# Rows on partitions: a first pass that convolves on TensorE, wide operands in the clustering, and attention in factored form

## The chip, the cores and the metric

The kernel runs on one core of a Trainium2 chip. The metric is the device time of one execution in microseconds, the median of several executions. The engines are TensorE (PE, with its weight loads shown apart as PEld), VectorE (DVE), ScalarE (ACT), GpSimd (POOL) and SyncE (SP), whose queue issues all the DMAs here.

## What is computed

The input x is 8 images of 512 channels of 128x128 float32, 268 MB. Two layers follow each other.

```python
# layer 0
x = conv(sx, w_down, stride 2, padding 1, groups of 2 channels)     # 8 x 256 x 64 x 64
labels = kmeans(normalised x[0], K=8, 10 iterations)                # over the 256 channels
v5 = mean of x over the channels of each cluster                    # 8 x 8 x 64 x 64
mu, var = gmm_fit(v5)                                               # 10 EM steps
pre_up = gate[:, slabel] * x + x                                    # gate from mu, var, w_conv
out0 = bilinear_up_x2(repeat(pre_up, 2, axis=1) * w_up) + sx
# layer 1; P is (128*128) x 64: products of 8 row and 8 column cosines
xP = einsum('bcn,nk->bck', x2, P)
WqxP, WkxP, WvxP = Wq @ xP, Wk @ xP, Wv @ xP
lamdq, lamdk = norms over o of (WqxP @ P.T), (WkxP @ P.T)           # one for every position
A = P.T @ (P / lamdk)                                               # 64 x 64, a sum over 16384 positions
out = ((A @ fatt) @ (P.T / lamdq) + P.sum(0)) / lamdv
out = gamma * (WvxP @ out + out_bias) + x
```

## The kernel before

Four parts follow each other, each a scope that ends with a barrier of all engines. A group of two input channels is convolved with its own 2x3x3 weights. T = 2 halves of 128 groups lie on the 128 partitions, and S = 2 is the channel within a group.

`first_pass` (L116) reads every image half in four chunks of 32 rows, a load of 4 MB each (L156), whose rows in memory are 16 KB long. The 18 taps of the convolution are 18 passes over a chunk: ACT makes the first (L282), DVE the other 17 (L217, a multiply and add that reads every second element), but for half of the fourth chunk, which POOL makes (L197 and L202). Beside that PE turns each row of x with the identity (L316), ACT copies the turned rows out of PSUM (L289), and PE multiplies them by `p_cols` (L328), which gives xP, the projection on the 64 cosine products. The two row blocks of L328 are written to the two halves of the output partitions in turn. The convolved rows go to the DRAM tensor `downsampled` (L170).

`gather_pass` (L364) reads `downsampled` back (L433), takes the same projection of it with transposes (L648) and products (L658), and runs k-means on image 0: PE makes a Gram matrix (L602), and 11 iterations of three small steps (L616, L622, L627) are threaded between the transposes, by the position numbers `ITER_AT` and so on. A step reads 8 columns. The averages of the clusters follow (L686). SP also issues here, in a list named `later`, the loads of tables for later use (L443). `mixture_pass` fits the mixture, on small operands.

`second_pass` (L1071) goes through the images in units of 4 rows, two units to a chunk of 8 rows. In a unit PE turns the interpolated rows and the cosine rows (L1336, L1349), DVE and POOL scale the turned rows (L1147), PE makes 16 products (L1366), and DVE adds them to x (L1607). SP stores each chunk in two DMAs of 1 MB (L1188) and loads another, three chunks ahead (L1180), into the buffer that a store has left. The attention numbers of the next image (`stage`) are made in the gaps between the units. There DVE and PE work over all 16384 positions: `norm_rows`, `norm_columns` (L1256, L1262, with L1516, L1526, L1529 on DVE), then `over_lam` and `over_positions` (16 DVE products L1536, 128 PE products L1270). For the first image they stand alone, ahead of the first unit.

Of the kernel before, what the change touches and what calls it, by code (L numbers as in the profile page):

```python
# [31 lines left out]
for _name, _width in CONST_COLS:  # L32
    CONST_AT[_name] = slice(CONST_N, CONST_N + _width)
    CONST_N += _width

# [52 lines left out]
TAPS = [(s, dh, dw) for dw in (0, -1, 1) for dh in (-1, 0, 1) for s in range(S)]  # L88
ROWS1 = 32
CH1 = H // ROWS1  # L90
TAPS_LEFT = len(TAPS) - 1
OUT1 = ROWS1 // 2
QUADS = S * ROWS1 // 4
SLOTS = 4
TP_BANKS = 2
UNROLL1 = 4
POOL_CHUNK = 3
FIRST_TAPS = [0, QUADS, 2 * QUADS, 2 * QUADS + 2]
STEPS = [TAPS_LEFT, TAPS_LEFT, TAPS_LEFT, 2 * TAPS_LEFT]


def weight_of(s, dh, dw):

    k = s * 9 + (dh + 1) * 3 + dw + 1
    return slice(k, k + 1)


def tap_window(buf, tap, rows, row0=0):

    s, dh, dw = tap  # L110
    top = 1 + dh + 2 * row0
    left = dw if dw >= 0 else 1
    return buf[:, s, top:top + 2 * rows - 1:2, left:left + 2 * (WD - (dw < 0)) - 1:2]


def first_pass(nc, x, w_down, p_cols, consts, cst, xd, xps):  # L116

    xv = x.rearrange("b (t g s) h w -> (b t) g s (h w)", t=T, s=S)
    with Scope(nc, "first") as sc:
        xt = [sc.sb(f"x{c}", [P, S, ROWS1 + 1, W]) for c in range(CH1)]  # L120
        wd = sc.sb("wd", [P, T, S * 9])
        p_sb = sc.sb("p", [P, H, UV])
        acc = [sc.sb(f"acc{i}", [P, OUT1, WD]) for i in range(CH1)]
        xT = [sc.sb(f"xT{i}", [P, 4, P]) for i in range(SLOTS)]
        tp = [sc.ps(f"tp{i}", [P, 4, P]) for i in range(TP_BANKS)]
        freq_ps = [sc.ps(f"freq{t}", [P, 512]) for t in range(T)]
        sum_ps = [bank[:, S * P:S * P + S * UV] for bank in freq_ps]
        product = sc.sb("product", [P, OUT1 // 2, WD])
        partial = [sc.ps(f"partial{i}", [P, OUT1, WD]) for i in range(2)]
        halves = sc.sb("halves", [P, S * P])  # L130
        const_in, p_in = sc.sem("const_in"), sc.sem("p_in")
        x_in = [sc.sem(f"x_in{c}") for c in range(CH1)]
        pe_read = [sc.sem(f"pe_read{c}") for c in range(CH1)]
        top_zero = sc.sem("top_zero")
        started = sc.sem("started")
        tapped = [sc.sem(f"tapped{c}") for c in range(CH1)]
        upper_tapped = sc.sem("upper_tapped")
        stored = [sc.sem(f"stored{i}") for i in range(CH1)]
        transposed = sc.sem("transposed")
        copied = [sc.sem(f"copied{i}") for i in range(SLOTS)]  # L140
        multiplied = [sc.sem(f"multiplied{i}") for i in range(SLOTS)]
        freq_read, folded, sum_read = sc.sem("freq_read"), sc.sem("folded"), sc.sem("sum_read")
        ident, fold = cst[:, CONST_AT["ident"]], cst[:, CONST_AT["fold"]]
        quads = CH1 * QUADS

        with nc.Block() as block:
            @block.sync
            def _(sp):
                sp.dma_start(cst[:, :], consts).then_inc(const_in, 16)
                sp.dma_start(wd[:, :, :], w_down.rearrange("(t g) s a b -> g t (s a b)", t=T)).then_inc(const_in, 16)  # L150

                def load(i, c):

                    sp.wait_ge(pe_read[c], i + FREE)
                    above = 1 if c == 0 else 0
                    sp.dma_start(xt[c][:, :, above:, :].rearrange("g s h w -> g s (h w)"),  # L156
                                 xv[i, :, :, (c * ROWS1 - 1 + above) * W:(c + 1) * ROWS1 * W]
                                 ).then_inc(x_in[c], 16)

                for c in range(CH1):  # L160
                    load(0, c)
                    if c == 0:
                        sp.dma_start(p_sb[:, :, :], p_cols.rearrange("w (h k) -> w h k", k=UV)).then_inc(p_in, 16)

                def store(i, c):

                    sp.wait_ge(tapped[c], i * STEPS[c] + STEPS[c] + FREE)
                    if c == POOL_CHUNK:
                        sp.wait_ge(upper_tapped, i * TAPS_LEFT + TAPS_LEFT + FREE)
                    sp.dma_start(xd.rearrange("b t g n -> (b t) g n")[i, :, c * OUT1 * WD:(c + 1) * OUT1 * WD],  # L170
                                 acc[c][:, :, :].rearrange("g h w -> g (h w)")).then_inc(stored[c], 16)

                start_free(sp, stored)
                with sp.Fori(0, B * T - 1) as i:
                    for c in range(CH1):
                        store(i, c)
                        load(i + 1, c)
                for c in range(CH1):
                    store(B * T - 1, c)
                for c in range(CH1):  # L180
                    sp.wait_ge(stored[c], B * T * 16 + FREE)

            @block.gpsimd
            def _(pool):
                nc.gpsimd.memset(xt[0][:, :, 0, :], 0.0).then_inc(top_zero, 1)
                start_free(pool, [tapped[POOL_CHUNK]])
                c, rows = POOL_CHUNK, slice(OUT1 // 2, OUT1)
                for i in range(B * T):
                    done = i * STEPS[c] + FREE
                    pool.wait_ge(x_in[c], i * 16 + 16)  # L190
                    pool.wait_ge(started, i * CH1 + c + 1)
                    for n, (s, dh, dw) in enumerate(TAPS[1:]):
                        left = 1 if dw < 0 else 0

                        if n > 0 or i > 0:
                            pool.wait_ge(tapped[c], done + 2 * n)
                        nc.gpsimd.tensor_scalar(product[:, :, left:],  # L197
                                                tap_window(xt[c], (s, dh, dw), OUT1 // 2, OUT1 // 2),
                                                wd[:, i % T, weight_of(s, dh, dw)], None, ALU.mult
                                                ).then_inc(tapped[c], 1)  # L200
                        pool.wait_ge(tapped[c], done + 2 * n + 1)
                        nc.gpsimd.tensor_tensor(acc[c][:, rows, left:], acc[c][:, rows, left:], product[:, :, left:],  # L202
                                                ALU.add).then_inc(tapped[c], 1)

            @block.vector
            def _(dve):
                dve.wait_ge(top_zero, 1)
                start_free(dve, [*tapped[:3], upper_tapped])

                def tap(t, c, n, rows, mine):  # L210
# [847 lines left out]
PIECES = 16  # L1058
PKBUF = 4
FACTORS = UNITS - 3  # L1060
SET_UP = 5

# [718 lines left out]
```

## Time and profile before

| | us |
|---|---|
| median of 3 runs | 3322.35 (3321.49 to 3327.83) |
| profiled execution, its own time | 3323.32 |
| its span | 3321.5 |
| PE busy in the span | 2942.4 |
| DVE busy | 2716.8 |
| ACT busy | 1839.0 |
| POOL busy | 1431.5 |
| moved by DMA | 946.92 MB |

The span counts from the first instruction to the last one. Busy times are of whole stages and say nothing of what a stage waits for. For that the stages are taken one by one, by the engine and by the share of time in which the DMA engines had packets.

### The profile page before, as it was taken

What the parts mean: (1) busy time and instruction counts of PE and PEld (TensorE: products, weight loads), DVE (VectorE), ACT (ScalarE), POOL (GpSimd) and SP (SyncE); (2) the same over time, 40 slices, a digit from 0 to 9 for tenths busy, and PEclk for the clock granted to TensorE, in tenths of its full rate; (3) what the DMA queues carried; (4) which work ended last, traced back from release to release, by engine and by line L of the source; (5) the groups of instructions that cost most, each with busy time, mean ns of one, the idle gap of its engine ahead of it and who ended that gap; (6) DMA issues with size and microseconds to landing.
All of it is one profiled execution on the core that took longest, in us unless ns stands there. A gap on an engine that the chain in (4) does not pass through costs nothing. (4 is left out here: it accounts for less than half of the span.)

```text
span 3321.5 us, 62992 instructions
## 1 busy us (share of the span) xinstructions
PE 2942.4 (89%) x23398; PEld 2260.2 (68%) x23398; DVE 2716.8 (82%) x3454; ACT 1839.0 (55%) x4385; POOL 1431.5 (43%) x805
## 2 busy tenths in 40 slices
PE   6898989898899985998586899999999999999997
PEld 4565656565555553763343798888889898888887
DVE  4999999899999994110554898989999998989997
ACT  4455555555555554122231767676766767676675
POOL 1676766666677772000000334343343434334443
PEclk9899999899999997769797999999999999999999
DMA  6667666756556645245003799999999999999999
GB/s 266 262 257 283 245 248 262 278 227 268 233 233 249 274 190 199 102 181 194 6 0 146 279 372 391 377 383 386 377 384 371 390 374 390 375 382 390 377 412 392
DMA packets 190885, 946.92 MB, mean 285 GB/s; under 512 B 13505, under 2 KB 13633, under 8 KB 170626
## 3 DMA queue, kind: packets, MB, share of 16 engines
q1 hardware_dynamic: 190594, 943.04, 73.2%
q8 instruction: 183, 3.00, 0.4%
q14 instruction: 108, 0.88, 0.1%
HBM read 638.90 MB, written 301.99 MB: 283 GB/s over the span
## 5 line engine op out<-in xcount | busy, mean ns | idle before, releaser
L1147 POOL TENSOR_TENSOR second_left<-second_mid_copy,second_coef_rep 64x1024 f32<-64x1024 f32 x256 | 606.2, 2368 | 1435.6 <-ACT second_mid_copy L1473 1405.2
L1366 PE MATMUL second_o<-second_right,second_left 128*128 128x128 f32 x8192 | 1065.6, 278 | 84.9 <-issue 28.7
L1366 PEld LDWEIGHTS second_o<-second_right,second_left 128*128 128x128 f32 x8192 | 978.9, 192 | 138.8 <-issue 109.7
L217 DVE SCALAR_TENSOR_TENSOR first_partial<-first_x,first_wd,first_partial 128x1024 f32<-128x1024 f32 (+1 forms) x960 | 1015.6, 1175 | 0.0
L1607 DVE SCALAR_TENSOR_TENSOR second_x<-second_o,second_shift,second_x 128x512 f32<-128x512 f32 x1024 | 724.7, 736 | 121.9 <-PE second_o L1366 117.8
L289 ACT ACTIVATE first_xT<-first_tp 128x512 f32<-128x512 f32 x1024 | 566.8, 596 | 439.3 <-PE first_tp L316 437.0
L316 PE MATMUL first_tp<-all_const,first_x 128*128 128x128 f32 x4096 | 592.1, 288 | 137.2 <-ACT first_xT L289 91.9
L316 PEld LDWEIGHTS first_tp<-all_const,first_x 128*128 128x128 f32 x4096 | 454.7, 145 | 346.2 <-issue 227.0
L197 POOL TENSOR_SCALAR first_product<-first_x,first_wd 128x512 f32<-128x512 f32 (+1 forms) x272 | 465.5, 1712 | 415.7 <-ACT first_acc L282 390.5
L328 PE MATMUL first_freq<-first_xT,first_p 128*64 128x256 f32 x4096 | 565.5, 399 | 0.0
L202 POOL TENSOR_TENSOR first_acc<-first_acc,first_product 128x512 f32<-128x512 f32 (+1 forms) x272 | 359.3, 1321 | 22.7
L328 PEld LDWEIGHTS first_freq<-first_xT,first_p 128*64 128x64 f32 x4096 | 254.9, 139 | 166.6 <-issue 92.9
L1452 ACT ACTIVATE second_mid<-second_dd,all_inter 128x128 f32<-128x128 f32 x1024 | 313.3, 389 | 7.6 <-DMA second_dd<-downsampled 4.4
L1452 ACT ACTIVATE second_part<-second_dd,all_inter 128x128 f32<-128x128 f32 x1024 | 313.3, 389 | 3.2
L1147 DVE TENSOR_TENSOR second_left<-second_mid_t,second_coef_rep 64x1024 f32<-64x1024 f32 x256 | 308.7, 1206 | 0.9 <-PE second_mid_t L1336 0.6
L1473 ACT ACTIVATE second_mid_copy<-second_mid_t 64x512 f32<-64x512 f32 x256 | 151.7, 593 | 266.8 <-PE second_mid_t L1336 266.1
L566 ACT ACTIVATE gather_dT<-gather_tp 128x512 f32<-128x512 f32 x128 | 76.4, 598 | 202.1 <-PE gather_tp L648 201.9
L1588 DVE TENSOR_TENSOR second_mid<-second_mid,second_part 128x1024 f32<-128x1024 f32 x128 | 172.6, 1348 | 3.5 <-ACT second_part L1452 3.5
L1336 PE MATMUL second_mid_t<-all_const,second_mid 128*128 128x128 f32 x1024 | 161.0, 280 | 15.9 <-DVE second_mid L1588 15.9
L217 DVE SCALAR_TENSOR_TENSOR first_partial<-first_x,first_wd,first_acc 128x1024 f32<-128x1024 f32 x64 | 85.4, 1363 | 97.2 <-ACT first_acc L282 95.6
L1476 ACT ACTIVATE second_right<-second_zt_t 64x256 f32<-64x256 f32 x256 | 96.6, 377 | 119.9 <-PE second_zt_t L1349 119.2
L282 ACT ACTIVATE first_acc<-first_x,first_wd 128x512 f32<-128x512 f32 x128 | 98.2, 767 | 93.1 <-DMA first_x<-in_x 93.1
(236 smaller groups left out, 2272.6 us busy)
## 6 DMA issues: line engine op xcount, KB each, us to landing
second_x<-in_x SPq DMA_DIRECT2D x256, 1024.0 KB, 12.8
out<-second_x SPq DMA_DIRECT2D x256, 1024.0 KB, 11.7
first_x<-in_x SPq DMA_DIRECT2D x48, 4224.0 KB, 18.5
first_x<-in_x SPq DMA_DIRECT2D x16, 4096.0 KB, 15.3
gather_d<-downsampled SPq DMA_DIRECT2D x24, 2048.0 KB, 12.2
downsampled<-first_acc SPq DMA_DIRECT2D x64, 512.0 KB, 3.9
second_dd<-downsampled SPq DMA_DIRECT2D x64, 512.0 KB, 13.6
first_p<-in_p_cols SPq DMA_DIRECT2D x1, 4096.0 KB
```

The lines of the kernel that those rows point to most:

```text
L197: nc.gpsimd.tensor_scalar(product[:, :, left:], tap_window(xt[c], (s, dh, dw), OUT1 // 2, OUT1 // 2), wd[:, i % T, weight_of(s, dh, dw)], ...
L202: nc.gpsimd.tensor_tensor(acc[c][:, rows, left:], acc[c][:, rows, left:], product[:, :, left:], ALU.add).then_inc(tapped[c], 1)
L217: return nc.vector.scalar_tensor_tensor(out=after[:, rows, left:], in0=tap_window(xt[c], (s, dh, dw), count, row0), scalar=wd[:, t, weight ...
L289: nc.scalar.activation(xT[slot][:, :, :], tp[q % TP_BANKS][:, :, :], ACT.Copy).then_inc(copied[slot], 1)
L316: last = nc.tensor.transpose(tp[q % TP_BANKS][:, n * S + s, :], xt[c][:, s, 1 + r + n, :], ident)
L328: last = nc.tensor.matmul(freq_ps[t][n * UV:(n + 1) * UV, 0:S * P], p_sb[:, row, :], xT[slot][:, n * S:(n + 1) * S, :].rearrange("p s g -> ...
L1147: return eng.tensor_tensor(left[a][rows, odd:HALF:2, :, :].rearrange("p n (t s) g -> p n t s g", t=T), turned[rows, :, :, :].unsqueeze(3). ...
L1336: last = nc.tensor.transpose(mid_t[:, n, t, :], mid[m % 2][:, t, r:r + 2, :].rearrange("p h w -> p (h w)"), k("ident"))
L1366: last = nc.tensor.matmul(ob[n][:, r, :], left[a][:, r, n, :], right[a][:, r, :], start=True, stop=True)
L1452: last = nc.scalar.activation((mid[c], part)[r][:, :, 2 * i + 1 - e, :], dd[:, :, row(i + e + r - 1), :], ACT.Copy, scale=row_w[:, 2 * e + ...
L1588: nc.vector.tensor_tensor(mid[c][:, :, :, :], mid[c][:, :, :, :], part[:, :, :, :], ALU.add).then_inc(interpolated, 1)
L1607: nc.vector.scalar_tensor_tensor(out=xt[i][:, n // S, n % S, rows, :], in0=ob[n][:, :, :], scalar=shift[:, n:n + 1], in1=xt[i][:, n // S, ...
```

## The change

In the first pass a load is now one group of channels, for all images: a partition holds two neighbouring rows of one channel, for each of the 8 images, in pieces of 1 KB (1 MB a load, 256 loads, 14 buffers). POOL builds for each group a band matrix of the weights for every column tap. PE convolves by 6 products per group (L241) of 504 or 512 columns each, the two groups of a pair in turn to the two halves of the output partitions. It projects the rows of four groups by 16 products of 32 output partitions (L257). ACT copies the convolved rows out, and SP stores them in pieces of 256 B. DVE finishes the projection over the columns by one product and one sum of 4096 elements per partition for every four groups. xP goes through a new DRAM tensor `projected`, and comes back in 16 loads of `later`, in pieces of 32 B. In k-means the moving operand is read 16 times over, which makes 128 columns of 8. In the attention the sums over positions are taken in factors: over columns, then over rows, with tables of products of cosines. The table `att_cols` (959 KB) is loaded first in the second pass, and both PE and DVE wait for it.

```diff
+    xv = x.rearrange("b (c s) (i r) w -> c (s i) b (r w)", s=S, r=2)
+    xdv = xd.rearrange("b t g (h w) -> (t g h) b w", w=WD)
...
+                def load(unit):
+
+                    if unit >= SLOTS1:
+                        sp.wait_ge(freq_made, (unit - SLOTS1) // GROUP1 + 1)
+                    sp.dma_start(xt[unit % SLOTS1][:, :, :, :].rearrange("p b r w -> p b (r w)"), xv[unit]
+                                 ).then_inc(x_in[unit % SLOTS1], 16)
...
+                for g in range(GROUPS1):
+                    for pair in (2 * g, 2 * g + 1):
+                        store(pair)
+                    for unit in range(g * GROUP1 + SLOTS1, (g + 1) * GROUP1 + SLOTS1):
+                        if unit < UNITS1:
+                            load(unit)
...
+                    for unit in units:
+                        nc.gpsimd.tensor_tensor(
+                            band[unit % WEIGHTS1][:, :, :, :], shift[:, :, :].unsqueeze(2).broadcast_to([P, 3, 3, HD]),
...
+                        nc.gpsimd.tensor_tensor(b[:, 2, :, :], b[:, 2, :, :], b[:, 0, :, :], ALU.add).then_inc(banded, 1)
...
+                    nc.vector.tensor_tensor(
+                        product[:, :, :, :], freq_ps[g % FREQ_BANKS][:, :, :].unsqueeze(2).broadcast_to(shape),
+                        cols[:, :, :].unsqueeze(1).broadcast_to(shape), ALU.mult).then_inc(freq_taken, 1)
+                    dve.wait_ge(freq_taken, g + 1)
+                    nc.vector.tensor_reduce(freq[:, g, :, :], product[:, :, :, :], AX.X, ALU.add
+                                            ).then_inc(freq_summed, 1)
...
+                def convolve(pair):
+
+                    bank = conv_ps[pair % CONV_BANKS]
+                    if pair >= CONV_BANKS:
+                        pe.wait_ge(conv_copied, pair - CONV_BANKS + 1)
+                    pe.wait_ge(banded, 2 * pair + 2)
+                    for n, (r, dw) in enumerate(TAPS):
+                        left = 1 if dw < 0 else 0
+                        at = dw + 2 * left
+                        for e in range(2):
+                            unit = 2 * pair + e
+                            if n == 0:
+                                pe.wait_ge(x_in[unit % SLOTS1], (unit // SLOTS1 + 1) * 16)
+                            last = nc.tensor.matmul(bank[e * HD:(e + 1) * HD, :, left:],
+                                                    band[unit % WEIGHTS1][:, 1 + r, dw + 1, :],
+                                                    xt[unit % SLOTS1][:, :, r, at:at + 2 * (WD - left) - 1:2],
+                                                    start=n == 0, stop=n == len(TAPS) - 1)
+                    last.then_inc(conv_made, 1)
...
+                            last = nc.tensor.matmul(bank[32 * q:32 * q + 32, :, :], rows[:, r, j, :],
+                                                    xt[unit % SLOTS1][:, half * HALF_B:(half + 1) * HALF_B, r, :],
+                                                    start=n == 0, stop=n == 3)
...
+                        for t in range(T):
+                            last = nc.tensor.matmul(repeats(count_ps[:, 0:P]), ones, repeated(oh[:, t, :]),
+                                                    start=t == 0, stop=t == T - 1)
...
+                    for m in range(LOW):
+                        last = nc.tensor.matmul(st[:, 2 * UV:2 * UV + W],
+                                                grams_u[:, m, :, :].rearrange("p a l -> p (a l)"),
+                                                pairs("pair_w")[:, m * W:(m + 1) * W],
+                                                start=m == 0, stop=m == LOW - 1)
+                    last.then_inc(u_summed, 1)
...
+                    for v in range(LOW):
+                        last = nc.tensor.matmul(st[0:UV, 0:UV], pairs("place_u")[:, v * UV:(v + 1) * UV],
+                                                weighted_v[:, v, :, :].rearrange("p l m -> p (l m)"),
+                                                start=v == 0, stop=v == LOW - 1)
+                    last.then_inc(a_made, 1)
...
+        later = [(xps[:, b * T + t, :, :].rearrange("g s (u v) -> g (s u) v", v=LOW),
+                  by_group[t, b // HALF_B, b % HALF_B]) for b in range(B) for t in range(T)]
```

On PE, the first pass began with turned rows of x and their products with `p_cols`, in the kernel before:

```order
4 L316 MATMUL first_tp<-all_const,first_x 128x128 x8
5 L313 REGISTER_ALU
6 L316 MATMUL first_tp<-all_const,first_x 128x128 x8
7 L324 REGISTER_ALU
8 L328 MATMUL first_freq<-first_xT,first_p 64x256 x4
9 L316 MATMUL first_tp<-all_const,first_x 128x128 x8
10 L328 MATMUL first_freq<-first_xT,first_p 64x256 x4
```

Now PE has two pairs of groups convolved and then four groups projected, and so on 64 times:

```order
1 L241 MATMUL first_conv<-first_x,first_band 64x512 x8
2 L241 MATMUL first_conv<-first_x,first_band 64x8x63 x4
3 L241 MATMUL first_conv<-first_x,first_band 64x512 x8
4 L241 MATMUL first_conv<-first_x,first_band 64x8x63 x4
5 L257 MATMUL first_freq<-first_x,first_rows 32x512 x16
6 L241 MATMUL first_conv<-first_x,first_band 64x512 x8
7 L241 MATMUL first_conv<-first_x,first_band 64x8x63 x4
```

The transposes are gone, and the convolution has come to PE. In SP's queue, at the start of the gather part, stood in the kernel before:

```order
31 L435 DMA gather_q<-in_q_cols 128x2048
32 L433 DMA gather_d<-downsampled 128x4096 x4
33 L443 DMA all_inter<-in_inter_cols 128x384
34 L443 DMA all_r<-in_r_cols 64x1024
35 L443 DMA all_wqk<-in_wqk 128x512
36 L443 DMA all_wv<-in_wv 128x2048
```

Now, at the same place, SP has:

```order
134 L351 DMA all_const<-in_consts 128x1212
135 L352 DMA gather_q<-in_q_cols 128x2048
136 L349 DMA gather_d<-downsampled 128x4096 x4
137 L360 DMA all_xps<-projected 128x16x8 x16
138 L360 DMA all_inter<-in_inter_cols 128x384
```

The 16 loads of xP stand between the loads of images 0 and 1 and that of image 2.

## Rows read from the trace of the kernel before

**Rows 1.** Stages: length; busy PE, PEld, DVE, ACT, POOL; granted clock, DMA share, GB/s
```profile
0.00:1268.00 1268.00, 1099.64 (x8256) 716.62 (x8256) 1161.37 (x1088) 656.89 (x1186) 825.29 (x549) 0.94 0.63 248
1268.00:1588.00 320.00, 282.87 (x1682) 170.35 (x1682) 58.65 (x192) 97.15 (x195) 0.00 (x0) 0.80 0.45 173
1588.00:1766.00 178.00, 128.16 (x1124) 68.12 (x1124) 113.05 (x322) 54.25 (x99) 0.00 (x0) 0.86 0.00 0
1766.00:1835.00 69.00, 45.39 (x333) 29.09 (x333) 27.20 (x46) 17.07 (x45) 2.34 (x1) 0.67 0.44 175
1835.00:3144.00 1309.00, 1236.76 (x10763) 1133.46 (x10763) 1199.76 (x1608) 895.08 (x2528) 528.27 (x223) 1.00 0.99 377
3144.00:3321.00 177.00, 149.59 (x1244) 142.57 (x1242) 156.78 (x200) 118.51 (x333) 75.55 (x32) 0.97 1.00 404
```

**Rows 2.** Costliest groups of the page: first pass, on DVE and POOL
```profile
L217 DVE SCALAR_TENSOR_TENSOR first_partial<-first_x,first_wd,first_partial 128x1024 f32<-128x1024 f32 (+1 forms) x960 | 1015.6, 1175 | 0.0
...
L202 POOL TENSOR_TENSOR first_acc<-first_acc,first_product 128x512 f32<-128x512 f32 (+1 forms) x272 | 359.3, 1321 | 22.7
```

**Rows 3.** Stretches with rows of 16 KB, mixed, 4 KB and 2 KB in flight
```profile
1275.00:1281.00 6.00, 0.00 (x0) 0.00 (x0) 3.29 (x1) 0.00 (x0) 0.00 (x0) 0.50 1.02 437
3180.00:3300.00 120.00, 109.77 (x909) 104.61 (x908) 113.38 (x144) 88.14 (x255) 56.11 (x25) 0.99 1.03 417
3301.00:3312.00 11.00, 8.35 (x71) 7.95 (x70) 8.43 (x12) 1.35 (x3) 2.60 (x2) 1.00 1.00 409
1768.00:1771.00 3.00, 3.00 (x4) 0.73 (x4) 0.00 (x0) 0.00 (x0) 0.00 (x0) 0.50 0.83 263
```

**Rows 4.** DMA view of 3.8 to 4.3 us, where the weights load in 72 B pieces
```profile
DMA packets 209, 0.15 MB, mean 309 GB/s; under 512 B 194, under 2 KB 194, under 8 KB 203
...
q1 hardware_dynamic: 209, 0.15, 151.8%
```

**Rows 5.** PE in order of time in the first pass: start, length
```profile
604.30 1.08 PE L328 MATMUL first_freq<-first_xT,first_p 128*64 128x256 f32 x8
605.32 1.09 PE L316 MATMUL first_tp<-all_const,first_x 128*128 128x128 f32 x8
```

**Rows 6.** Groups of the gather stage: count, busy us, mean ns
```profile
L602 PE MATMUL gather_gram_ps<-gather_d 128*128 128x256 f32 x128 | 29.7, 385 | 0.0
...
L686 PE MATMUL gather_gram_ps<-gather_d,gather_placed 128*32 128x512 f32 x128 | 14.5, 594 | 0.0
...
L481 DVE TENSOR_REDUCE gather_lo<-gather_d 128x1 f32<-128x4096 f32 x2 | 8.8, 4408 | 0.0
```

**Rows 7.** Gather stage in order of time: loads, image 2's first transposes, k-means early, late
```profile
1268.37 15.10 SPq L433 DMA_DIRECT2D gather_d<-downsampled  x4
...
1334.52 0.60 PE L648 MATMUL gather_tp<-all_const,gather_d 128*128 128x128 f32 x4
...
1365.27 1.06 PE L616 MATMUL gather_x<-gather_wt,gather_gram 128*128 128x8 f32 x8
...
1371.38 1.06 PE L616 MATMUL gather_x<-gather_wt,gather_gram 128*128 128x8 f32 x8 [0.38 <-DVEq L528]
...
1437.75 1.88 PE L616 MATMUL gather_x<-gather_wt,gather_gram 128*128 128x8 f32 x8
...
1447.46 1.88 PE L616 MATMUL gather_x<-gather_wt,gather_gram 128*128 128x8 f32 x8
```

**Rows 8.** Granted clock in the late iterations
```profile
1375.00:1470.00 95.00, 95.00 (x393) 62.81 (x390) 25.62 (x147) 18.51 (x34) 0.00 (x0) 0.50 0.43 177
```

**Rows 9.** What the SP queue waited for, 1835 to 3144 us
```profile
SPq L1188 <- DVE second_x L1607: 858.6, 112, 61.8
```

**Rows 10.** What the SP queue waited for, 3144 to 3321 us
```profile
SPq L1180 <- DMA out<-second_x: 78.9, 25, 5.8
```

**Rows 11.** First image's attention, in order of time: on ACT, then DVE
```profile
1776.92 0.32 ACT L1420 ACTIVATE second_grams<-second_st 64x192 f32<-64x192 f32 x1 [0.89 <-PE second_st L1248]
...
1815.75 0.28 DVE L1566 SCALAR_TENSOR_TENSOR second_a_free<-all_const,second_a 64x64 f32<-64x64 f32 x1 [3.29 <-ACT second_a L1427]
```

More of the change, by code:

```diff
@@ L83, in sem @@
         return self.sems[-1]
[L88 to L93, printed above, removed]
-SLOTS = 4
[L95 to L113, printed above, removed]
@@ L160, in _ @@
[L160 to L171, printed above, removed]
@@ new lines, in store, with store_freq @@
+                def store(pair):
+                    sp.wait_ge(conv_copied, pair + 1)
+                    sp.dma_start(xdv[pair * P:(pair + 1) * P], staged[pair % STAGED][:, :, :]
+                                 ).then_inc(stored[pair % STAGED], 16)
+                def store_freq(first, last):
+                    sp.wait_ge(freq_summed, last)
+                    for half in range(2):
+                        for m in range(GROUP1):
+                            at = half * 64 + m * 16
+                            sp.dma_start(xpv[half, m, :, first:last, :],
+                                         freq[at:at + 16, first:last, :, :].rearrange("p n c v -> p n (c v)")).then_inc(freq_out, 16)
@@ L183, in _ @@
+                store_freq(GROUPS1 // 2, GROUPS1)
+                for i in range(STAGED):
+                    sp.wait_ge(stored[i], pairs // STAGED * 16)
+                sp.wait_ge(freq_out, 2 * 2 * GROUP1 * 16)
             @block.gpsimd
             def _(pool):
[L185 to L203, printed above, removed]
@@ L297, in _ @@
+                for pair in range(pairs):
+                    act.wait_ge(conv_made, pair + 1)
+                    if pair >= STAGED:
+                        act.wait_ge(stored[pair % STAGED], pair // STAGED * 16)
+                    nc.scalar.activation(staged[pair % STAGED][:, :, :], conv_ps[pair % CONV_BANKS][:, :, :], ACT.Copy
+                                         ).then_inc(conv_copied, 1)
             @block.tensor
             def _(pe):
-                start_free(pe, [*multiplied, *pe_read])
@@ L353 @@
+                for g in range(GROUPS1):
+                    convolve(2 * g)
+                    convolve(2 * g + 1)
+                    project(g)
 RING = 4
@@ L1726, in shape_constants @@
                                 [np.tile(np.asarray(v, f), (P, 1)) for v in (above, below, here, under)], 1)
-    r = np.zeros((LOW, LOW, H, LOW), f)
-    for v in range(LOW):
-        r[:, v, :, v] = d.T
-    r_cols = r.reshape(UV, H * LOW)
     row = np.arange(P)
+    pair = (d[:, :, None] * d[:, None, :]).astype(f)
+    side, high, low = row // UV, row // LOW % LOW, row % LOW
+    own, at = row // HD, row % HD
+    halo = np.stack([at[:, None] + 1 == np.arange(HD)[None, :]] + [at[:, None] == np.arange(HD)[None, :]] * 2, 1)
+    turned = np.stack([[d[2 * at + r][:, None, :] * (2 * j + own[:, None, None] == np.arange(4)[None, :, None])
+                        for j in range(2)] for r in range(2)]).transpose(2, 0, 1, 3, 4)
+    first = {"shift": halo, "rows": turned, "cols": np.tile(d.T.reshape(1, -1), (P, 1))}
+    first_cols = np.concatenate([np.asarray(first[n]).astype(f).reshape(P, w) for n, w in FIRST_COLS], 1)
+    attention = {
+        "own_u": (side * LOW + high)[:, None] == np.arange(2 * LOW)[None, :],
+        "pair_w": pair[:, low, :].transpose(1, 2, 0),
+        "pair_h": (side[:, None] == np.arange(2)[None, :])[:, :, None] * pair[:, high, low].T[:, None, :],
+        "pair_v": pair,
+        "place_u": d[:, None, :, None] * np.eye(LOW)[None, :, None, :],
+    }
+    att_cols = np.concatenate([np.asarray(attention[n]).astype(f).reshape(P, w) for n, w in ATT_COLS], 1)
     rb, rf, rk = row // 16, row // 8 % 2, row % 8
```

466 lines of the change are left out of this document (184 added, 282 removed).

## The prediction

> **What bounds the kernel now.** I read the stages first [rows 1]. The first pass takes 1268 us. DVE is busy for 1161 of them, its long group of taps never waited [rows 2], and the DMA engines had packets for 0.63 of the time only: DVE sets the pace, at a rate of 248 GB/s. The gather stage (320 us) is PE's, busy 283 us at a mean clock of 0.80. The mixture (178 us) is not touched by the change. The first image's attention stands alone (69 us). Then seven images take 1309 us, 187.0 each, and the last one 177 us with its drain. In the seven, PE and DVE are busy 177 and 171 us per image, and SP waited for DVE before its stores [rows 9]. In the last image, which makes no attention numbers for a next one, DVE needs 157 us, and there SP waited mostly for stores to land before it could load [rows 10], at 417 GB/s [rows 3]. So the second pass is engine bound while it makes attention numbers, and DMA bound as soon as it does not.
>
> **The first pass: what DMA will need.** It moves 268 MB in pieces of 1 KB and 33.5 MB out in pieces of 256 B. Such pieces are not in the trace. Pieces of 16 KB ran at 437 / 1.02 = 428 GB/s, 612 ns each on one of 16 engines, and those of 4 KB at 409 GB/s, 160 ns [rows 3]. The line through both is 9.5 ns plus 0.0368 ns per byte: 47 ns for 1 KB, 19 ns for 256 B, 11 ns for 32 B. From the other side: 2 KB pieces at the start of the second pass took 16 x 2048 / (263 / 0.83) = 103 ns [rows 3], where the line says 85; a line through that and 4 KB gives 75 ns for 1 KB. And 194 small packets (72 B) went in 0.5 us over 16 engines, at most 41 ns each [rows 4]. I take 47 ns for 1 KB, since the 4 KB row is a long steady stream and the 2 KB row a short start, and 25 ns for 256 B, nearer to the line since the 41 is from a start too. Four groups then cost each DMA engine 4 x 64 x 47.3 + 2 x 64 x 25 ns = 12.1 + 3.2 = 15.3 us.
>
> The Trainium skill (DMA: Bandwidth & Descriptors, Specifications) says that pieces under 512 B cost a read, modify and write. No row shows it for stores to memory. If it doubled the line's 19 ns to 38, the stores would need 4.9 us per four groups in place of 3.2, which puts the first pass 106 us later. It speaks against this change, and my 25 ns lies between.
>
> **The first pass: the engines beside it.** A product in the program is two records on PE. A record of 256 columns that has the array to itself takes 29.7 / 128 = 0.232 us [rows 6], so 0.464 for 512. Records that alternate between the two halves overlap: eight of 256 columns fill 1.02 us [rows 5], 0.128 each, where the weight loads may already set the pace. Four strips overlap wholly: 14.5 / 128 = 0.113 us per 512 columns [rows 6]. So a pair of groups is 24 x 0.232 = 5.6 us (6.1 by the ratio of rows 5), and four groups are 11.2 + 32 x 0.113 = 14.8 us (15.9). DVE has two instructions of 4096 elements, 2 x 4.41 = 8.8 us [rows 6]. POOL has 4 x 768 elements at 1321 / 512 ns, 7.9 us [rows 2]. ACT has two copies, 1.2 us. None of the three decides while DMA needs 15.3. SP sends a group's two stores ahead of four loads, and the loads wait for PE (`freq_made`), but ten loads, some 30 us of data, are in the queue behind that wait. I take 64 x 15.3 = 979 us, plus 9 us until the tables and the first group are there, plus 20 us at the end (a convolution, a projection, DVE, the last stores): 1008 us, **260 less**. The removed work (18 taps, transposes, their copies) is all inside the 1268.
>
> **Gather.** Of 11 k-means iterations the first took 6.1 us from start to start, and a late one 9.7 [rows 7]: in between the clock had fallen from 2.4 to 1.2 GHz while PE was busy without a break, with short 8-column matmuls among its work [rows 8]. The wide operands fill these records. If the clock stays up, 95 us become 95 x 6.1 / 9.7 = 60: 35 less. Eight records of 8 columns fill 1.06 us [rows 7] and eight of 128 columns 1.09 us (L316 [rows 5]), so the width itself costs nothing. The constants now load here, 2 us. The 16 loads of xP are 2048 pieces of 32 B for each engine, 11 to 41 ns each; I take 20, 41 us. They stand in the queue after image 1, which was issued by 1283.5 [rows 7] and needs 10 us, and ahead of 4 us of tables and of image 2 (10 us). That lands at 1294 + 41 + 14 = 1349, in the old time, and PE wants it at 1334.5 [rows 7]: 15 us late, and k-means is behind it on PE. Between 0 and 52 by the two prices. Sum: **18 less**.
>
> **The second pass.** For image 0, from the Gram copy to the free row of A, 38.8 us passed [rows 11]. The new chain has twelve short steps: a DVE product of 1024 elements, 16 PE records of 128 columns at the low clock (3.5 us), copies, root, reciprocal, 16 records of 64 columns. I estimate 12 us, so 27 less; 959 KB of `att_cols` must land first, with PE and DVE held at their first instruction, 3 more: **24 less**. In the seven images the removed work is 15 us of DVE (171 against 157) and 27 of PE (177 against 150) [rows 1], and about 5 us of each comes back. The engines would then need some 162 us, but an image moves 68 MB (2^20 B), 71.3 MB, which at 417 GB/s is 171 us. I take 172.5, since the two bind at nearly the same time: 7 x 14.5 = **101 less**. Bounds: 171 (112 less), 180 (49 less). The last image stays.
>
> **Sum.** 3323.3 - 260 - 18 - 24 - 101 = 2920 us, in the terms of the profiled execution, which lies 1 us above the median. The span is 2 us shorter.
>
> **The rivals.**
> (a) Small pieces at the line's price: DMA needs 14.5 us per four groups, PE's 14.8 binds, the first pass takes 976 us, and xP is not late. 2920 - 32 - 15 = 2873; with a PE that is better than the rows, 2835. For it: the line fits two long streams. Against: nothing this small was streamed. 0.18.
> (b) Dearer pieces: 1 KB between 50 and 75 ns, or 256 B at 41. At 17.4 us per four groups (256 B at 41) it is 2920 + 131 + 37 = 3088; at 20 us 3258. For it: the 2 KB row. 0.20, mostly under 3150.
> (c) Slower than before: the six products of a group do not overlap with those of its neighbour. The moving operand is now read with a step of two elements, from two different tiles, and a third of the results start one column into the bank; no PE record in the trace does either. Four groups are then 4 x 12 x 0.464 + 3.6 = 25.9 us, the first pass 1687, the whole 3600. It decides above 21.6 us per four groups, where the first pass has eaten all 403 us. DVE read steps of two at no loss (1175 ns for 1024 elements [rows 2], as 4096 contiguous ones take 4408 [rows 6]). 0.07.
> (d) The images lie 32 MB apart in memory, and each DMA engine hops over all eight for every row pair. If that halves the rate of the loads, they need 24.2 us per four groups, with the stores 27.4, and the whole is 3694. Loads of x now have rows 128 KB apart and run at full rate; no row has hops of megabytes. 0.06. The Trainium skill (DMA: Bandwidth & Descriptors, Latency and other measured facts) has half rate for rows at a pitch of 4 MiB and more.
> (e) The attention or the clock gives nothing: the clock falls in spite of the wide operands (35 more), or the seven images stay at 180 us (52 more): 2955 to 3007. 0.09.
>
> **How the numbers follow.** The forecast has 0.40. With (a), (e) and two thirds of (b) the range from 2835 to 3170 holds 0.80. A measurement tells 0.2% from no change. Faster: 0.40 + 0.18 + 0.09 + 0.18 of (b) = 0.85; slower 0.14, from (c), (d) and an end of (b); same 0.01.
>
> **What would show it.** In the first pass of the changed kernel: DMA share near 1.00 at about 310 GB/s, PE waiting for x, DVE and POOL under 0.65 busy. If PE is busy throughout and DMA is not, (a) or (c) holds, told apart by records per microsecond of L241. In gather: clock 1.00 through k-means, iterations at 6.1 us, and PE's wait at image 2. In the seven images: SP waiting for stores to land, not for DVE, and 416 GB/s. It is wrong if the first pass is not within 975 to 1090 us.

## The result, and the profile after

The changed kernel takes 2973.99 us (median, 2971.82 to 2980.78) beside 3325.09 us for the kernel before on the same chip: a ratio of 0.8945, 95% interval 0.8923 to 0.8967. The forecast was 2920 us, with a range of 2835 to 3170. The time lies in the range and 54 us above the forecast, and the sum hides misses that go against each other: 99 us in the images one way, 48 us ahead of them the other way. The span of the profiled execution fell from 3321.5 to 2970.0 us, 351.5 less.

The stages of the changed kernel, with the columns of [rows 1] (length; busy PE, PEld, DVE, ACT, POOL; granted clock, DMA share, GB/s):

```profile
0.00:971.00 971.00, 941.48 (x5120) 285.61 (x5120) 566.07 (x128) 77.75 (x129) 432.30 (x516) 0.99 0.99 315
971.00:1262.00 291.00, 245.60 (x1682) 146.05 (x1682) 58.63 (x192) 97.16 (x195) 0.00 (x0) 0.93 0.56 196
1262.00:1440.00 178.00, 127.30 (x1124) 68.09 (x1124) 112.96 (x321) 54.23 (x99) 0.00 (x0) 0.87 0.00 0
1440.00:1485.00 45.00, 20.57 (x96) 13.74 (x96) 10.72 (x20) 17.26 (x46) 2.34 (x1) 0.65 0.72 290
1560.00:1860.00 300.00, 274.21 (x2288) 256.10 (x2287) 274.49 (x361) 226.81 (x638) 132.79 (x56) 1.00 1.03 415
1900.00:2800.00 900.00, 764.97 (x6132) 718.28 (x6132) 743.51 (x969) 606.96 (x1711) 357.84 (x151) 0.96 1.01 375
2779.00:2970.00 191.00, 146.36 (x1208) 138.48 (x1206) 148.75 (x190) 114.15 (x325) 73.45 (x31) 0.97 0.98 373
```

Against [rows 1]:

| | forecast | measured |
|---|---|---|
| first pass, 1268 us | -260 | -297 |
| gather, 320 | -18 | -29 |
| mixture, 178 | 0 | 0 |
| first image's attention, 69 | -24 | -24 |
| the eight images, 1486.5 | -101 | -2 |
| sum of the spans | -403 | -352 |

So the first pass and the gather stage gave more than was forecast, and the images gave nothing. The last three rows of the view above say when: until 1860 us the DMAs moved 415 GB/s, as the forecast wanted, and from 1900 on 375, at DMA shares of 1.03 and 1.01, with PE, DVE and ACT all less busy than before. The last row is the last image. DVE marks the start of each image by a small copy. The first, second, third, fourth and last of them, in order of time:

```profile
1480.38 0.15 DVE L1542 COPY second_shift<-second_next_shift 128x4 f32<-128x4 f32 x1
1654.62 0.17 DVE L1542 COPY second_shift<-second_next_shift 128x4 f32<-128x4 f32 x1
1828.62 0.17 DVE L1542 COPY second_shift<-second_next_shift 128x4 f32<-128x4 f32 x1
2013.49 0.17 DVE L1542 COPY second_shift<-second_next_shift 128x4 f32<-128x4 f32 x1
...
2778.93 0.17 DVE L1542 COPY second_shift<-second_next_shift 128x4 f32<-128x4 f32 x1
```

Two images took 174 us each, close to the forecast's 172.5. The third took 185, and the five from 2013 to the end at 2970 took 191 each, which is more than the 187 of the kernel before. What SP waited for in the images (from 1500 to 2880 us: in all, times, longest), and SP's stores early and late (duration of an issue in ns, and us from issue to landing, each as min/median/max):

```profile
SPq L1108 <- DMA out<-second_x: 862.3, 228, 6.4
SPq L1116 <- DVE second_x L1526: 81.2, 55, 10.3
```

```profile
L1116 SPq DMA_DIRECT2D out<-second_x x41: 582/673/1647, 1561.9 to 1775.1; - x41
DMA to landing us min/median/max: 10.3/15.4/16.2
...
L1116 SPq DMA_DIRECT2D out<-second_x x37: 582/835/3498, 1903.1 to 2119.8; - x37
DMA to landing us min/median/max: 16.0/17.4/19.0
```

SP waited for stores to land and not for DVE, as forecast (in [rows 9] it was DVE). But the landings came later and later.

### The profile page after: what moved, and what is told of

Same layout as the page of the kernel before. It is cut to its first block, busy times and chain, and to the rows that moved or that the text cites. A ratio compares the mean times of both kernels' runs of the same rounds, so it can differ in the third digit from the quotient of the medians.

```text
span 2970.0 us, 47824 instructions
## 1 busy us (share of the span) xinstructions
PE 2610.5 (88%) x18374; PEld 1710.4 (58%) x18374; DVE 2000.4 (67%) x2285; ACT 1261.3 (42%) x3336; POOL 1040.5 (35%) x772
## 4 chain that ended last, share of the span: by engine, by line
DMA 35%; PE 8%; DVE 3%; ACT 2%; issue 1%; SPq 1%; POOL 0%; DVEq 0%; ACTq 0%
DMA out<-second_x 27%; PE second_o L1302 6%; DMA second_dd<-downsampled 4%; DMA second_x<-in_x 3%; DVE second_x L1526 1%; DVE second_left L1075 1%; PE second_mid_t L1272 1%; SPq L1108 1%; ACT second_mid L1391 1%; PE second_st L1162 1%; DVE second_mid L1507 1%; ACT second_left L1403 0%; POOL second_left L1075 0%; ACT second_part L1391 0%; PE second_zt_t L1285 0%
## 5 line engine op out<-in xcount | busy, mean ns | idle before, releaser
L241 PE MATMUL first_conv<-first_x,first_band 128*64 128x512 f32 (+1 forms) x3072 | 717.4, 616 | 13.5 <-POOL first_band L200 10.6
L210 DVE TENSOR_TENSOR first_product<-first_freq,first_cols 128x4096 f32<-128x4096 f32 x64 | 283.2, 4425 | 395.7 <-PE first_freq L257 395.7
L241 PEld LDWEIGHTS first_conv<-first_x,first_band 128*64 128x64 f32 x3072 | 225.6, 135 | 499.0 <-issue 468.3
L193 POOL TENSOR_TENSOR first_band<-first_shift,first_w_all 128x576 f32<-128x576 f32 x256 | 289.9, 1154 | 493.3 <-PE first_conv L241 486.7
L223 ACT ACTIVATE first_staged<-first_conv 128x512 f32<-128x512 f32 x128 | 76.5, 597 | 873.6 <-DMA downsampled<-first_staged 648.8
L214 DVE TENSOR_REDUCE first_freq<-first_product 128x32 f32<-128x4096 f32 x64 | 282.9, 4420 | 2.2
L257 PE MATMUL first_freq<-first_x,first_rows 128*32 128x512 f32 x2048 | 233.0, 595 | 0.0
L1272 PEld LDWEIGHTS second_mid_t<-all_const,second_mid 128*128 128x128 f32 x1024 | 116.5, 143 | 119.6 <-DVE second_mid L1507 115.7
L257 PEld LDWEIGHTS first_freq<-first_x,first_rows 128*32 128x32 f32 x2048 | 60.0, 109 | 169.5 <-issue 169.5
L200 POOL TENSOR_TENSOR first_band<-first_band 128x192 f32<-128x192 f32 x256 | 147.8, 599 | 0.0
## 6 DMA issues: line engine op xcount, KB each, us to landing
first_x<-in_x SPq DMA_DIRECT2D x256, 1024.0 KB, 10.4
```

Source lines behind the costliest of these rows:

```text
L193: nc.gpsimd.tensor_tensor(band[unit % WEIGHTS1][:, :, :, :], shift[:, :, :].unsqueeze(2).broadcast_to([P, 3, 3, HD]), w_all[:, unit, :].re ...
L210: nc.vector.tensor_tensor(product[:, :, :, :], freq_ps[g % FREQ_BANKS][:, :, :].unsqueeze(2).broadcast_to(shape), cols[:, :, :].unsqueeze( ...
L214: nc.vector.tensor_reduce(freq[:, g, :, :], product[:, :, :, :], AX.X, ALU.add).then_inc(freq_summed, 1)
L241: last = nc.tensor.matmul(bank[e * HD:(e + 1) * HD, :, left:], band[unit % WEIGHTS1][:, 1 + r, dw + 1, :], xt[unit % SLOTS1][:, :, r, at:a ...
L257: last = nc.tensor.matmul(bank[32 * q:32 * q + 32, :, :], rows[:, r, j, :], xt[unit % SLOTS1][:, half * HALF_B:(half + 1) * HALF_B, r, :], ...
L1272: last = nc.tensor.transpose(mid_t[:, n, t, :], mid[m % 2][:, t, r:r + 2, :].rearrange("p h w -> p (h w)"), k("ident"))
```

## The experiments

e1, e4 and e9 were executed 4, 4 and 10 times, the other kernels once.

**Is it time that makes the images slow, or their place?** Two kernels: SP lets the queues run empty before every other image, or the images come in another order.

> The changed kernel, and SP waits at the start of images 2, 4 and 6 until all stores issued so far have landed. In the changed kernel the first two images took 174 us each at 416 GB/s, the later ones 185 to 195 at about 375. Theory A: something builds up in the DMA queues from one emptying to the next (the 16 DMA engines come apart, and a transfer has landed only when the slowest has done its part). Then each pair of images runs like the first two: 8 x 174 = 1392 us for the images in place of 1485, plus three waits of about 10 us, so 60 less than the changed kernel, about 2910 us, and the rate is back at 416 GB/s after each wait. Theory B: the later images lie at addresses, or the DMAs meet at a phase, that is slower in itself: nothing is won, the three waits are added, about 3000 us. Theory C: four buffers of x are too few for the way load, adding, store: also about 3000.

```
                 def step(b, u, more):
                     m = chunk_of(u)
+                    if u == 0 and b in (2, 4, 6):
+                        for i in range(XBUF):
+                            for t in range(T):
+                                sp.wait_ge(y_out[i][t], b * (CH2 // XBUF) * 16 + Y_LEAD)
```

2891.28 us (ratio to before 0.87, interval 0.8677 to 0.8724), 83 us under the changed kernel. Stretches between the waits of this kernel, then what SP waited for (L1136 is the new wait):

```profile
1560.00:1800.00 240.00, 220.09 (x1848) 207.19 (x1848) 222.28 (x290) 181.01 (x515) 107.13 (x46) 1.00 1.03 416
1900.00:2120.00 220.00, 197.09 (x1655) 185.02 (x1655) 197.81 (x258) 161.34 (x457) 96.31 (x41) 1.00 1.03 416
2220.00:2480.00 260.00, 232.95 (x1943) 219.25 (x1942) 234.61 (x305) 191.05 (x545) 114.14 (x48) 0.99 1.03 417
2600.00:2820.00 220.00, 188.94 (x1581) 178.68 (x1581) 193.90 (x252) 159.88 (x456) 96.79 (x41) 1.00 1.03 416
```

```profile
SPq L1136 <- DMA out<-second_x: 32.7, 6, 5.9
```

416 GB/s in each stretch. The three waits held SP for 32.7 us together, yet the images cost only about 2 us more than the first two, since, as the program reads, the engines still had loaded chunks of x in hand.

> The changed kernel, and the second pass goes through the images in the order 2, 3, 4, 5, 6, 7, 0, 1. Theory A (something builds up since the queues were last empty): still the first two in time at 174 us each and the others at about 190, the same total, 2974 us. Theory B (the addresses of the images): slow from the first image on, 190 us, and the last two, which are images 0 and 1, at 174; the total is the same, so the windows decide.

```
-                    rows = xd[b + j // LOADS].rearrange("t g n -> g t n")
+                    rows = xd[(b + j // LOADS + 2) % B].rearrange("t g n -> g t n")
...
-                                 xv[b + m // CH2, t, ...
+                                 xv[(b + m // CH2 + 2) % B, t, ...
```

2978.03 us. The first two images in time are fast again and the others slow:

```profile
1560.00:1800.00 240.00, 219.94 (x1848) 206.97 (x1847) 222.19 (x289) 181.17 (x517) 107.87 (x46) 1.00 1.03 416
1900.00:2800.00 900.00, 761.25 (x6127) 714.69 (x6128) 741.33 (x967) 605.95 (x1710) 356.16 (x150) 0.97 1.01 374
```

Theory B falls by both, and theory C by e1. Something builds up from the time when the queues were last empty.

> As e1, but SP waits at the start of every image but the first. Theory A: no image leaves the fast time; seven waits of 5 to 10 us, 8 x 174 + 50, about 2930 us, and 2890 if the waits are hidden by work that the engines have in hand. Theories B and C: about 3030.

The condition of e1 becomes `u == 0 and b > 0`. 2890.53 us (ratio 0.8697, interval 0.8674 to 0.872): the end of the expectation in which the waits are hidden. Twice as many waits gain nothing over e1, so two images are a close enough distance.

**Is it the number of buffers?**

> The changed kernel with five buffers of x in place of four, SP two more half chunks ahead. To make room, the table of cosine products for the second pass is cut to its upper half, so the lower half of every image is computed from the wrong rows of it, and 2 MB less is loaded. Theory A: the way of a buffer is longer by a chunk, so the slow time sets in later: 416 GB/s for about four images in place of two, and a total some 40 us less, 2930. Theory B: same as the changed kernel, 2974. Theory C (four buffers too few from the start): 416 GB/s throughout, 8 x 172, so about 2865.

```
-XBUF = 4
+XBUF = 5
...
-        p_sb = sc.sb("p", [P, H, UV])
+        p_sb = sc.sb("p", [P, H // 2, UV])
```

2971.56 us, and the slow time sets in as early. Both theories A and C had expected a gain. The order of the waits offers a reason why there was none: `AHEAD` is `XBUF - 1`, so SP still waited for the store of the chunk just before, and only four transfers were queued behind it.

> As e3 (five buffers, the lower half of the cosine table left out), but the loads are issued three chunks ahead as in the changed kernel, so a load waits for a store of one chunk earlier. In e3 the way was the same as with four buffers: SP still waited for the store that it had issued just before, with four transfers (10 us) queued behind it, and the slow time set in as early. Theory A, amended: the fast DMA engines run dry once the slowest is further behind than what is queued, 10 us. Here twice as much is queued, 20 us, so the fast time should last about twice as long, to 2150 to 2300 us, and the total be 30 to 50 less, 2925 to 2945. If the limit is in the queue itself and not in what the program holds ready: slow again from 1850 on, 2972.

```
-AHEAD = XBUF - 1
+AHEAD = 3
```

2889.95 us, from a kernel that leaves out the lower half of the cosine table. It is better than expected, and not in the way expected: 416 GB/s did not last to 2150 us or longer, it fell to about 410 from 1980 us on, and no deep slow time followed. The stretch from 1900 to 2800 us of e3 and then that of e5; after them, for e5 between 2000 and 2300 us, what SP waited for, and how long its issues of stores took (ns, min/median/max):

```profile
1900.00:2800.00 900.00, 766.97 (x6152) 724.18 (x6151) 748.07 (x970) 609.94 (x1722) 358.78 (x152) 0.95 1.01 376
```

```profile
1900.00:2800.00 900.00, 798.51 (x6653) 747.94 (x6654) 806.16 (x1050) 659.50 (x1865) 390.10 (x164) 1.00 1.02 409
```

```profile
SPq L1116 <- DVE second_x L1526: 53.4, 26, 4.5
SPq L1100 <- ACT second_part L1391: 13.4, 6, 4.1
```

```profile
L1116 SPq DMA_DIRECT2D out<-second_x x55: 583/2372/5161, 1996.1 to 2295.8; - x55
```

SP no longer waits for a store to land. An issue takes 2.37 us in the median where it took 0.67 in the changed kernel's fast time. We read that as full queues that hold SP, since a transfer of 1 MB at 409 GB/s takes 2.56 us. So the buffers as such were not short (e3); what counts is how much is queued behind the transfer that SP waits for. The three remedies e1, e4 and e5 end within 1.4 us of each other, at 175 to 176 us for each image from the third to the seventh, and e1 too moves 409 GB/s over 1900 to 2800 us once its waits are counted. Why they meet there is not shown.

No view lists the DMA engines one by one. But the trace holds the 16 landing marks of each transfer, one for each engine's part, and from them can be worked out how far the first and the last are apart (medians over 60 us). In the changed kernel it is 1.6 us at 1500, about 4 at 1620, 7.3 at 1740 and 9 to 10 from 1920 to 2800. Of those 9 to 10 us, 5 to 8 lie between the last mark and the one before it, so mostly one engine is late; the marks do not name it. In e1 it falls back from 7 or 8 to about 2 us at each wait. In e5 it also reaches 10 us, at 409 GB/s. In the kernel before, up to 3100 us, it stays under 4. Full load alone does not bring it: in the first pass of the changed kernel, 970 us at a DMA share of 0.99, it stays between 1.2 and 2.0 us. The Trainium skill (DMA: Bandwidth & Descriptors, Why a DMA increments its semaphore by 16 and not by 1) says that each engine of a transfer posts its own mark and only all 16 mean that the data landed. The marks agree: the 16 of one transfer come at different times. With some 10 us of lag and four transfers (10 us) behind the awaited one, the engines that are ahead would have nothing left when the last one lands, and with more queued they would. The trace's records of the single packets bear this out in part: in the changed kernel fewer than 16 are under way in 0.1% of the time from 1560 to 1740 us and in 12% from 1900 to 2800, and in e5 in 2% of that stretch. The typical packet of 4 KB takes 159 ns in both times; it is a few long ones (mean 160, then 176 ns) that keep the DMA share at 1.01.

**Was the kernel before held up by the same?**

> The kernel before, with the waits of e1 (SP waits at the start of images 2, 4 and 6 of the second pass until all stores have landed). If the seven images of before were bound by PE and DVE, as the prediction read them, they stay at 187 us and the waits add 0 to 10 us in all: 3325 to 3335. If they were held up by the DMA queues like the late images of the changed kernel, they come down towards 177 to 180 us, the busy time of PE: 50 less, about 3275.

The edit is that of e1. 3324.27 us, ratio 0.9996 (0.9985 to 1.0007). The seven images are the same to a hair, with 377 GB/s as in [rows 1]:

```profile
1835.00:3144.00 1309.00, 1236.45 (x10761) 1133.14 (x10762) 1199.84 (x1607) 897.66 (x2528) 527.89 (x223) 1.00 0.99 377
```

So emptying the queues gives them nothing, which fits the forecast's reading that the engines bound them. With e1 beside it, the lighter attention is worth about 11 us per image (187 against 176), once the queues are emptied.

**What sets the pace of the first pass?**

> The changed kernel with four of the six products in the convolution of the first pass (the left column tap is left out), so PE needs 14.5 - 3.7 = 10.8 us per four groups. If DMA set the pace of the first pass, as predicted: 971 us again. If PE set it (busy 941 of 971): it falls to what DMA needs, 14.5 us per four groups by the line's price (950 us), and less if small pieces are cheaper than the line.

```
-TAPS = [(0, 0), (1, 0), (0, 1), (1, 1), (0, -1), (1, -1)]
+TAPS = [(0, 0), (1, 0), (0, 1), (1, 1)]
```

2965.83 us. The start of the gather stage, which is SP's load of the constants, in the changed kernel and in e6, and then PE's waits in e6 from 100 to 900 us:

```profile
970.98 0.36 SPq L351 DMA_DIRECT2D all_const<-in_consts  x1
```

```profile
968.78 0.36 SPq L351 DMA_DIRECT2D all_const<-in_consts  x1
```

```profile
PE first_conv L241 <- DMA first_x<-in_x: 111.1, 85, 4.8
```

A quarter of PE's work gone gains nothing: in e1 to e5 and e8, which leave the first pass as it is, it ends between 968.7 and 972.1 us. DMA is at its limit, at 320 GB/s: 4.72 MB per four groups in 14.75 us. But PE is at its own in the changed kernel. From 100 to 900 us it waited for x for 2.3 us in all:

```profile
100.00:900.00 800.00, 797.67 (x4368) 243.12 (x4362) 481.14 (x109) 64.77 (x109) 367.80 (x436) 1.00 1.01 319
```

```profile
PE first_conv L241 <- DMA first_x<-in_x: 2.3, 2, 1.5
```

In the first 35 of 63 rounds it went from one set of four groups to the next in 14.53 us, without exception, with 14 loads of lead to live on; some later rounds are longer, and the mean of all is 14.67. So both limits lie within 2% of each other.

> The changed kernel, and each store of the first pass is made twice, the second time to a scratch tensor: 128 more pieces of 256 B on each DMA engine per four groups. If DMA is at its limit, the first pass grows by 64 x 128 x the price of such a piece: 155 us at 19 ns, 205 at 25 ns (the prediction), 336 at 41 ns. If they find room beside PE, less than 100.

```
-                    sp.dma_start(xdv[pair * P:(pair + 1) * P], staged[pair % STAGED][:, :, :]
-                                 ).then_inc(stored[pair % STAGED], 16)
+                    for rows in (xdv, again):
+                        sp.dma_start(rows[pair * P:(pair + 1) * P], staged[pair % STAGED][:, :, :]
+                                     ).then_inc(stored[pair % STAGED], 16)
```

3125.29 us. The first pass now ends at

```profile
1127.25 0.36 SPq L353 DMA_DIRECT2D all_const<-in_consts  x1
```

which is 158.5 us after that of e6, and 156.3 after that of the changed kernel, whose six products this one has. Divided by 64 x 128 pieces this is 19.3 or 19.1 ns for 256 B, the price of the line. The trace's own records of these pieces are 18 ns each. The rest of e6's 14.75 us, 14.75 - 2.47 = 12.28 us for 256 pieces of 1 KB, is 48 ns each, where the line says 47; the records of these pieces have a mean of 49.

**Do the wide operands hold the clock?**

> The changed kernel with the moving operand of k-means 8 columns wide, as before the change. Theory (the wide operands keep the clock up): the granted clock falls to 0.5 for some 95 us again, iterations of 9.7 us in place of 6.4, the gather stage 320 in place of 291, about 3003 us. Rival (the clock fell for another reason, such as what went before): iterations stay at 6.3 us and the total at 2974.

```
-WIDE = P // K
+WIDE = 1
...
-                    return bank.rearrange("p (a k) -> p a k", k=K)
+                    return bank[:, 0:WIDE * K].rearrange("p (a k) -> p a k", k=K)
```

2998.49 us. The stretch of k-means in the changed kernel, the same in this one, and one pair of iterations early and one late:

```profile
1070.00:1170.00 100.00, 92.59 (x664) 58.85 (x664) 30.16 (x170) 34.09 (x63) 0.00 (x0) 1.00 0.48 192
```

```profile
1070.00:1170.00 100.00, 98.63 (x453) 65.71 (x452) 27.89 (x159) 21.68 (x39) 0.00 (x0) 0.58 0.39 158
```

```profile
1077.99 1.06 PE L542 MATMUL gather_x<-gather_wt,gather_gram 128*128 128x8 f32 x8 [0.38 <-DVEq L446]
1084.10 1.06 PE L542 MATMUL gather_x<-gather_wt,gather_gram 128*128 128x8 f32 x8 [0.38 <-DVEq L446]
...
1142.35 1.88 PE L542 MATMUL gather_x<-gather_wt,gather_gram 128*128 128x8 f32 x8
1152.06 1.88 PE L542 MATMUL gather_x<-gather_wt,gather_gram 128*128 128x8 f32 x8
```

The mean granted clock of the stretch is 0.58 where it was 1.00, the late iterations, at the lower level, take 9.7 us, and the gather stage ends at 1291.2 in place of 1262.2, 29 us later. The theory holds. (The whole is 24.5 us longer than the changed kernel's median; the rest of this single run was shorter by the difference.)

## Why the forecast was right, and where it was wrong

The first pass paid for most of the gain, as forecast. That the sum came within 54 us is in part luck: the images gave 99 us less than forecast, and the first pass and the gather stage 37 and 11 more. With the images alone off it would have been 3019, still inside the range.

**The images: the step that failed.** The forecast took the 417 GB/s of [rows 3] as the rate at which an image moves, 171 us, for seven images in a row, and had the last image stay as it was. The rate is real: the first two images had it, 174 us each. But the row was read over 120 us, just after a long time in which the engines set the pace and the queues were not pressed. Under pressure the queues held 416 for about 350 us, and then 375: images of 191 us, the last one too, which before had taken 171 from its mark on DVE (at 3150.7) to the end. From the first mark to the last the seven images take 1298.5 us where they took 1320.6 before, 22 less, and the last one takes 20 more. So the term of -101 came out as -2. No rival named it; rival (e) had "the images stay at 180", a bound too kind by 11 us per image. That SP would wait for stores to land was forecast, but the forecast didn't ask how much is queued behind such a wait.

**The first pass: half right in its reading, one price too high.** DMA does set a floor, as e6 shows, the share is near 1.00 and the rate 315 to 319 GB/s, DVE and POOL are under 0.65 busy (566 and 432 of 971). But another sign of the forecast, PE waiting for x, did not come: PE waited 2.3 us of 800, and was as much at its limit as DMA. The price of 1 KB was right (47 taken, 48 measured). The 25 ns for 256 B was moved up from the line's 19 towards a bound of 41 from a start, and 19.3 was measured, which makes 64 x 128 x 5.7 ns = 47 us too many. That is rival (a)'s price, and its time for the stage, 976 us, is nearer than the forecast's 1008. The forecast had called itself wrong if the stage fell outside 975 to 1090; 971 is outside. (a)'s other half, that PE then decides, is not far off either: the two are 0.2 us per four groups apart, PE set the pace of the first half of the stage and DMA, by e6 the longer of the two, its end. No run with less DMA work shows how far PE alone would have come. Of the ten loads (30 us) that the forecast saw in the queue, about four were under way at a time: SP's loads landed 10.4 us after their issue in the median, and an issue took 2.45 us. Here that cost nothing. The doubling of small stores that was weighed (38 ns) did not show, and neither did a loss by the hops over the images, rival (d): 48 ns for 1 KB is within 2% of the line.

**PE's pairs overlap**, so rival (c) fell. Two rows of the page, and the work of four groups in order of time:

```profile
L241 PE MATMUL first_conv<-first_x,first_band 128*64 128x512 f32 (+1 forms) x3072 | 717.4, 616 | 13.5 <-POOL first_band L200 10.6
...
L257 PE MATMUL first_freq<-first_x,first_rows 128*32 128x512 f32 x2048 | 233.0, 595 | 0.0
```

```profile
612.14 3.64 PE L257 MATMUL first_freq<-first_x,first_rows 128*32 128x512 f32 x32
615.72 11.02 PE L241 MATMUL first_conv<-first_x,first_band 128*64 128x512 f32 x48
626.66 3.64 PE L257 MATMUL first_freq<-first_x,first_rows 128*32 128x512 f32 x32
```

717.4 / 3072 = 0.234 us per record, with steps of two elements and two different tiles (0.232 forecast), and 0.114 for the four strips (0.113). From one group of L257 to the next are 14.52 us; 14.8 was forecast.

**Gather.** The clock term held in kind: the ten steps from the first iteration to the last take 63.6 us (1074.66 to 1138.22) where they took 92.8, and e8, which gives the width back, gives 29 us back where 35 was forecast. An iteration takes 6.35 us, not the 6.1 of 8 columns at the same clock, so the width was not quite free. The price of the loads of xP was too high. PE was 2.2 us short before image 2, where 15 was forecast, and the first step of k-means came 103.7 us into the stage beside 97.3 [rows 7]:

```profile
1042.25 0.63 PE L576 MATMUL gather_tp<-all_const,gather_d 128*128 128x128 f32 x4 [2.25 <-issue]
...
1074.66 1.16 PE L542 MATMUL gather_x<-gather_wt,gather_gram 128*128 128x128 f32 x8
1125.52 1.16 PE L542 MATMUL gather_x<-gather_wt,gather_gram 128*128 128x128 f32 x8 [0.43 <-DVEq L446]
```

That is 6 us late in place of 17 (2 for the constants and 15), and even these do not show in the length of the stage: e8, with the new loads and the old width, has 320 us, as before the change. So the term of 17 came out as nothing and that of 35 as 29. What took the 6 us back behind k-means is not traced. SP needs 32 us to issue these 16 loads (988.0 to 1020.0), 15.6 ns for each of the 2048 pieces of 32 B, and image 2's load goes out at 1023.5. The 20 ns were an estimate between 11 and 41, and the lower end was the nearer one. (By the upper one the sum gives 58 us late and not the 52 of the forecast.)

**The first image's attention** was forecast at 24 less and gave 24: PE's first product of the images starts at 1485.1, 45 us into the pass. It is not by luck: the chain from the Gram copy to the free row of A took 11.6 us where 12 was estimated, and DVE and PE were held at the start until the table had landed:

```profile
1453.04 0.27 ACT L1355 ACTIVATE second_grams<-second_st 64x128 f32<-64x128 f32 x1 [0.55 <-PE second_st L1176]
...
1464.67 0.28 DVE L1485 SCALAR_TENSOR_TENSOR second_a_free<-all_const,second_a 64x64 f32<-64x64 f32 x1 [2.10 <-ACT second_a L1366]
```

**Open:** why the last landing falls behind by some 2.4 us in 100 us in the fast time of the second pass and not at all in the first pass, and why the rate is 375 and not 409 afterwards. e5 puts the second on the depth of the queue, and the packets under way fit that, but no view shows the engines singly. Nor is it shown what makes the difference in the first pass, where the pieces are smaller and eight of nine bytes are loads. There fewer than 16 packets are under way in 20% of the time at a steady lag, so that count is no proof by itself.

## What to carry to other kernels

A DMA rate read from a short stretch is not a rate for a millisecond: where loads wait for stores to land, look at how many transfers are queued behind the awaited one, and at whether the time from issue to landing grows. If it does, let the queues run empty now and then (here three waits gained 83 us of 2974), or wait for an older store, where a buffer more can be had for it. And price small pieces by a line through long, steady streams, without a surcharge taken from a start.

## What the hardware showed that was not expected

In the second pass the landings of one transfer came apart by 9 to 10 us over some 450 us, and the stream fell from 416 to 375 GB/s at a DMA share of 1.01, so the share alone hardly shows it; in the first pass, at a share of 0.99, they stayed within 2.0 us. With more transfers queued the same lag went with 409 GB/s. An issue on SP took 0.67 us in the changed kernel's fast time and 2.37 us in e5. Pieces of 256 B stored to memory cost 19.3 ns each on one engine (18 in the packet records), and pieces of 1 KB, loaded with hops of 32 MB between them, 48 ns.
